# Two staging buffers instead of four for the output pass, and a reordered scale row in the layer norm

## What is computed

```python
xn = layernorm(x)
# attention branch
q, k, v = split(xn @ w_qkv.T + b_qkv)          # 16 heads of 64
kv  = einsum('bhnd,bhne->bhde', softmax(k, axis=-2), v)
out = layernorm(einsum('bhnd,bhde->bhne', silu(q), kv)) * ln_g + ln_b
out = out * sigmoid((xn @ w_g1.T + b_g1) @ w_g2.T + b_g2)
attn = out @ w_out.T + b_out
# expert branch: 8 experts, top 2 of xn @ Wr.T, capacity 769 tokens
ffn = sum over the two chosen experts of weight * (xn @ We[e])
y = x + attn + ffn
```

## Time and profile before

| | |
|---|---|
| runs before | 1159.05 us median of 3 (1157.73 to 1199.94) |
| the profiled execution | 1157.35 us |
| its span, slowest core (6) | 1155.5 us, cores 1149.5 to 1155.5 |
| TensorE busy | 873.5 us, 76% of the span |
| VectorE, ScalarE, GpSimd busy | 39%, 9%, 5% |
| experts, start to last matmul | 695 to about 1138 us |
| first store to the end | 1089.44 to 1155.5 us |

### The profile page before, as it was taken

The page is one execution under the profiler, slowest core; times in us unless marked ns, Lnnn a source line. Parts: engine busy times, 40 slices in busy tenths (PEclk is TensorE's granted clock), DMA queues, the critical chain, the costliest instruction groups (busy, mean ns, idle before and its releaser), DMA issues.

```text
span 1155.5 us, 11082 instructions; the slowest of 8 cores (1149.5 to 1155.5 us)
## 1 busy us (share of the span) xinstructions
PE 873.5 (76%) x3848; PEld 357.2 (31%) x3914; DVE 449.6 (39%) x692; ACT 103.6 (9%) x123; POOL 57.9 (5%) x58
## 2 busy tenths in 40 slices
PE   0143072599997999651555999999999999999993
PEld 0010021133335433110101334444444444444441
DVE  0123767300332001736685334444444444444441
ACT  0111100122000221141221000000000000000000
POOL 2100000000000000000000000000000000000253
PEclk9986576699997899575556999999999999999997
DMA  2566600000404002200001004040404132231176
GB/s 48 115 173 152 106 1 1 1 1 1 73 1 74 1 1 35 39 0 0 1 0 55 19 1 73 1 73 1 73 5 69 21 54 33 41 49 24 49 234 227
DMA packets 23300, 55.59 MB, mean 48 GB/s; under 512 B 4752, under 2 KB 4752, under 8 KB 22224
## 3 DMA queue, kind: packets, MB, share of 16 engines
q0 software_dynamic: 16160, 29.68, 16.1%
q1 hardware_dynamic: 4208, 12.63, 3.7%
q10 hardware_dynamic: 2880, 12.58, 2.9%
HBM read 76.18 MB, written 8.39 MB: 73 GB/s over the span
## 4 chain that ended last, share of the span: by engine, by line
PE 62%; DVE 17%; DMA 13%; issue 4%; ACT 2%; DVEq 1%; POOL 0%; POOLq 0%; ACTq 0%
PE PS L168 62%; DMA ar<-x_fm 6%; DVE scr_b L178 5%; DVE ar L178 5%; DVE srow L178 3%; DMA y<-bpool 2%; DMA y<-reps 1%; DMA y<-fpool 1%; DVE reps L178 1%; ACT bpool L185 1%; DMA wg_sb<-wg_t 1%; ACT qrow L185 1%; DVEq L177 1%; DVE qrow L178 0%; DVE drow L178 0%
## 5 line engine op out<-in xcount | busy, mean ns | idle before, releaser
L168 PE MATMUL PS<-ar 128*128 128x512 bf16 (+1 forms) x3135 | 698.8, 377 | 21.2 <-DVE ar L178 9.8
L168 PEld LDWEIGHTS PS<-ar 128*128 128x128 bf16 x3200 | 302.6, 99 | 382.8 <-issue 53.1
L178 DVE SCALAR_TENSOR_TENSOR ar<-PS,lc,ar 128x512 bf16<-128x512 f32 x256 | 192.2, 751 | 251.1 <-PE PS L168 251.1
L178 DVE CAST ar<-PS 128x512 bf16<-128x512 f32 x96 | 66.4, 692 | 168.9 <-PE PS L168 165.7
L168 PE MATMUL PS<-ar,ones_c_b 128*1 128x512 bf16 x64 | 22.3, 484 | 91.4 <-ACT bpool L185 91.1
L185 ACT ACTIVATE ar<-PS 128x512 bf16<-128x512 f32 x64 | 38.2, 597 | 94.4 <-PE PS L168 94.4
L199 POOL DMA_DIRECT2D ar<-we x8 | 7.0, 876 | 663.0 <-PE PS L168 663.0
L168 PE MATMUL PS<-bpool,wg_sb 64*128 64x512 bf16 x32 | 18.7, 584 | 28.0 <-DVE ar L178 28.0
L168 PEld LDWEIGHTS PS<-ar,ones_c_b 128*1 128x1 bf16 x64 | 5.2, 92 | 106.9 <-issue 104.5
L185 ACT ACTIVATE bpool<-ar 128x2048 bf16<-128x2048 bf16 x16 | 30.6, 1910 | 84.9 <-DMA ar<-x_fm 40.0
L168 PE MATMUL PS<-bias_b,ones_b 1*128 1x512 bf16 x96 | 37.3, 389 | 0.3
(11 more groups left out here) (113 smaller groups left out, 304.3 us busy)
## 6 DMA issues: line engine op xcount, KB each, us to landing
ar<-we POOLq DMA_DIRECT2D x8, 2048.0 KB, 16.7
fpool<-x_fm SPq DMA_DIRECT2D x4, 1024.0 KB, 9.9
ar<-x_fm POOLq DMA_DIRECT2D x8, 512.0 KB, 7.1
bpool<-x_fm ACTq DMA_DIRECT2D x4, 1024.0 KB, 7.0
bpool<-x_tm SPq DMA_DIRECT2D x8, 512.0 KB, 4.2
y<-bpool ACTq DMA_DIRECT2D x8, 512.0 KB, 3.9
ar<-wk_t POOLq DMA_DIRECT2D x1, 2048.0 KB, 16.5
ar<-wv_t POOLq DMA_DIRECT2D x1, 2048.0 KB, 15.3
```

What stands on the lines that cost most here:

```text
L168: i = eng.matmul(out, l, r, start=start, stop=stop)
L178: getattr(eng, name)(*a, **k).then_inc(S["dv"], 1)
```

## The change

The output pass has two staging buffers, `fpool` and a new tensor `fpool2` of its own, in place of four. All distances of 4 tiles become 2: the load of tile tc waits for the add of tc - 2, the add of tile tc for the store of tc - 2. The first load waits for the end of the router's use of `fpool` only. In stage 1 `fpool2` takes the f32 slices that `bp1f` took.

`erow` is gone. The row phase computes mean * r in f32 into `qrow` and then -1 times it into `crow`; TensorE makes the columns from `crow` while it holds the mean, and the sign is put in as `nmu_c` is read. In the first norm the columns wait only for r, the write of `crow` waits for the columns, and the second four steps of `reps` wait for `crow`. `totr` and `offr` lie in `srow`, and the memset of `offr` moves from the program's start to a place after the first norm on GpSimd.

```diff
+        fpool2 = sb("fpool2", [128, 2048], F32)
-        bp1f = bpool1[:].rearrange("p a b -> p (a b)").bitcast(F32)
...
-        erow = sb("erow", [1, T], BF16)
...
-        totr = sb("totr", [1, NT * E], F32)
-        offr = sb("offr", [1, NT * E], F32)
+        totr = srow[0:1, 0:NT * E]
+        offr = srow[0:1, NT * E:2 * NT * E]
...
-                gps("memset", eps_sb[:], EPS, inc=False)
-                t_const_gp = gps("memset", offr[:, 0:E], 0.0)
+                t_const_gp = gps("memset", eps_sb[:], EPS)
...
-                    fbuf = fpool[:, :] if h % 2 == 0 else bp1f
+                    fbuf = fpool[:, :] if h % 2 == 0 else fpool2[:, :]
...
                 dve("reciprocal", srow[:], qrow[:], inc=False)
-                dve("tensor_copy", drow[:], srow[:], inc=False)
-                dve("tensor_scalar_mul", erow[:], crow[:], -1.0, inc=False)
-                t_rows = dve("tensor_mul", crow[:], erow[:], drow[:])
-                w("tensor", "dv", t_rows)
+                t_r_bf = dve("tensor_copy", drow[:], srow[:])
+                w("tensor", "dv", t_r_bf)
...
-                    mm(bank(2)[:, NT + tc:NT + tc + 1], erow[0:1, 128 * tc:128 * (tc + 1)],
+                    mm(bank(2)[:, NT + tc:NT + tc + 1], crow[0:1, 128 * tc:128 * (tc + 1)],
                        ones_b[0:1, 0:1], start=True, stop=True, inc=(tc == NT - 1))
                 t_cols_pe = c["pe"]
+                dve("tensor_mul", qrow[:], crow[:], drow[:], inc=False)
+                w("vector", "pe", t_cols_pe)
+                t_rows = dve("tensor_scalar_mul", crow[:], qrow[:], -1.0)
                 w("vector", "pe", t_cols_pe)
                 dve("tensor_copy", r_c[:], bank(2)[:, 0:NT], inc=False)
-                t_cols_ev = dve("tensor_copy", nmu_c[:], bank(2)[:, NT:2 * NT])
+                t_cols_ev = dve("tensor_scalar", nmu_c[:], bank(2)[:, NT:2 * NT],
+                                -1.0, None, op0=ALU.mult)
...
+                        if which == 1 and tb == 0:
+                            w("tensor", "dv", t_rows)
...
+                w("gpsimd", "dv", t_r_bf)
+                t_offz = gps("memset", offr[0:1, 0:E], 0.0)
...
+                w("vector", "gp", t_offz)
                 dve("tensor_copy", totr[:], bank(6)[0:1, 0:128], inc=False)
...
-                dve("tensor_scalar_mul", erow[:], crow[:], -1.0, inc=False)
-                t_rows2 = dve("tensor_mul", crow[:], erow[:], drow[:])
+                dve("tensor_mul", qrow[:], crow[:], drow[:], inc=False)
+                t_rows2 = dve("tensor_scalar_mul", crow[:], qrow[:], -1.0)
...
-                pbs = (fpool[:, :], bp1f, repsf, bp2f)
+                pbs = (fpool[:, :], fpool2[:, :])
...
                 w("sync", "dv", t_lgt_hl)
-                w("sync", "pe", t_lrawT_pe)
-                w("sync", "pe", t_st2_pe)
-                w("sync", "dv", t_zg)
...
-                    pb = pbs[tc % 4]
-                    if tc >= 4:
-                        w("sync", "gp", add_toks[tc - 4])
+                    pb = pbs[tc % 2]
+                    if tc >= 2:
+                        w("sync", "gp", add_toks[tc - 2])
...
-                    if tc >= 4:
-                        w("gpsimd", "d3", out_toks[tc - 4])
+                    if tc >= 2:
+                        w("gpsimd", "d3", out_toks[tc - 2])
```

More of the change, by code:

```diff
@@ L762, in program @@
                 t_moe = c["dv"]
-                repsf = reps[:].rearrange("p a b -> p (a b)").bitcast(F32)
-                bp2f = bpool2[:].rearrange("p a b -> p (a b)").bitcast(F32)
-                pbs = (fpool[:, :], bp1f, repsf, bp2f)
+                pbs = (fpool[:, :], fpool2[:, :])
                 out_toks = {}
```

## The result

The changed kernel takes 1163.25 us (median of 11 runs), the kernel before 1158.48 us beside it; the ratio is 1.0046, 95% interval 1.0033 to 1.0059, so +5.3 us (+3.8 to +6.8). The forecast was 1163.5 us, made of +5.9 us. The profiled execution has a span of 1159.9 us on its slowest core (4); the cores lie between 1151.8 and 1159.9.

The account below looks back on a forecast made before the run. The output pass was taken as bound by its store queue, one transfer in flight; -0.2 + 0.4 + 1.6 + 4.1 = +5.9 us on the profiled 1157.35 us gave 1163.3, forecast as 1163.5 us, range 1157.0 to 1170.5.

Parts of the forecast that it names:

- The start, -0.2: GpSimd's queue of small loads: one memset leaves ahead of its first transfer, -0.2 us, ends -0.6 and 0.
- First norm, +0.4: First norm's rows: 3.41 us become 3.80, with a 2.28 us product covering TensorE's columns, +0.4 us.
- Second norm, +1.6: Second norm: same exchange of rows with nothing to cover it while TensorE waits for `crow`, +1.6 us.
- Rival four: Norms: the product costs 1.21 us, giving 1161.2 us; its chance is counted in the forecast's 0.53.
- Sum ahead of the pass +1.8: Start and both norms, before the output pass: -0.2 + 0.4 + 1.6 = +1.8 us.
- Two more stores with a load beside them, +3.1: Output pass: two more stores take 4.51 us beside a load instead of 2.98 alone, +3.1 us.
- The coupling, +1.0: Output pass: slow transfers that four buffers took up must be passed on by two, +1.0 us, between 0 and 3.1.
- The check from the other side: Output pass: 14 loads in a row lead to an end at 1157.2, the stores to 1158.5; chains meet within 1.3 us.
- Two buffers suffice for the mean durations: Output pass: load and store each have 2.2 us to spare, so the store queue stays the bound.
- rival three: Output pass: one buffer's load, add and store fall in series, +23.6 us, in all 1182.8 us; chance 0.04.
- The first two `x_tm` loads early, the rows in `srow`, `fpool2` in stage 1, costed at 0: Router rows and stage 1: loads start near 197 us without other transfers, rows and `fpool2` keep sizes; cost 0.
- lockstep: Output pass: add k releases load k + 2 and often store k together, +12.2 us, in all 1171.4 us; chance 0.16.

Follow-up runs that it names:

- Norm_bf16: Changed kernel with the product of mean and r written as bf16, not f32, in both norms: ratio 1.0017, +2.0 us against the kernel before.
- norm_only: Changed kernel with the four staging buffers and distances of 4 put back: ratio 1.0018, +2.1 us against the kernel before.
- late_loads: Kernel before, four buffers kept, but the loads of tiles 2 and 3 wait for the adds of tiles 0 and 1: ratio 1.0024, +2.8 us.
- the two experiments with fewer loads: Adds in place: changed kernel's two buffers as four slots, ratio 1.0018; kernel before's four buffers as eight slots, ratio 0.9952, both against the kernel before.
- tail_only: Kernel before with two staging buffers in the output pass and nothing else changed: ratio 1.0033, +3.8 us.
- two_stores: Kernel before with stores on two counters in turn, so two may be in flight: ratio 0.9967, -3.8 us.
- after_two_both: Changed kernel, still two buffers, with two loads and two stores in flight: ratio 1.0003, +0.3 us against the kernel before.
- two_both: Kernel before with two stores and two loads in flight, two counters on each queue: ratio 0.9925, -8.7 us.

## Why the prediction was right

Step by step, by the terms of the sum:

- The start, -0.2: the first transfer is issued at 3.13 us and not at 3.33. Right; what of it reaches the end was not measured.
- First norm, +0.4: 3.41 us became 3.80. Second norm, +1.6: TensorE's wait went from 33.58 to 35.18. Right to 0.1 us, since the product took the 2.28 us of the row with the same result type. Norm_bf16 shows that the type is the cause. Rival four is out.
- Sum ahead of the pass +1.8: the first add is 1.7 us later on the mean core, and norm_only costs +2.1 us (+0.8 to +3.4). Counted from the first `reciprocal`, four kernels with the changed norms reach the first add after 962.7 to 963.2 us and four with the norms of before after 960.5 to 961.1: 2.3 us for the 2.0 of the two norms.
- Two more stores with a load beside them, +3.1: 14 stores at 4.52 us and two short ones. Right as a mechanism by late_loads and by the two experiments with fewer loads.
- The coupling, +1.0: not found. On all eight cores the first 14 stores follow one another with no gap over 0.4 us, and from the first issue to the last landing they take 4.39 us each on average, where the first 12 took 4.43 before (in tail_only 14 take 4.46). On core 4 the pass of 71.2 us is 2.9 us over the 68.3 us of core 6 before, which the 3.1 us cover alone. The step that was oversized is the estimate of what a slow load does; the spare time worked out just before it (2.2 + 2.2 us) was the better guide, and loads on core 4 were not slow, 4.9 us at most against 6.0 on core 6 before. By the times of late_loads and tail_only alone it could still be 1 us or a little more; by the store rows it is 14 x 0.03 = 0.4 us.
- The check from the other side, that the loads' chain nearly meets the stores': it does not bind here, but it was the right thing to look at, for it is what stopped two_stores.
- "Two buffers suffice for the mean durations": right, as long as one transfer at a time is in flight, and wrong in after_two_both. The series of rival three, priced with load, add and store, did not occur; what occurs with full queues is the shorter round of add and store.
- The first two `x_tm` loads early, the rows in `srow`, `fpool2` in stage 1, costed at 0: nothing in norm_only beyond the norms' own 1.8 us.

The forecast's 1163.5 us also rests on a little luck: +1.0 for the coupling is too much, and the forecast notes that the median of the runs lies 1.7 us above the profiled execution but then adds 0.2 us to the sum for it. With the 1.7 it would have been 1165.0, so the two slips partly cancel. One reading was off without an effect: against lockstep it gives the later stores beside loads 4.4 us on average, and the stores of tiles 2 to 11 took 4.2, which speaks against that rival a little more.

## What to carry to other kernels

Before counting buffers, ask how many transfers a queue has in flight. With one at a time, as here, the waits between buffers were hidden behind the queue, and what fewer buffers really cost was the early loads that they pushed into the busy stretch. Price it by the same transfer's two durations, alone and in company, which the tail of one profile shows side by side. And where a row on one partition is on the path, the type of an intermediate result counts as much as the number of instructions: take the price from the row whose result has the same type.

## What was not expected of the hardware

- On core 6 of the kernel before, loads of 512 KB take 3.5 to 4.0 us to land with nothing beside them, stores 2.6 to 3.2, and with one of each in flight their medians are 4.2 and 4.3. With two of each in flight (two_both) the medians differ by core, 4.9 to 6.6 us for loads and 5.2 to 6.4 for stores. From 1100 to 1130 us cores 0, 4 and 6 move 228 to 247 GB/s before and 295 to 303 in two_both, where I had feared that 260 was the limit.
- The cores fall in two groups long before the pass: the first `reciprocal` starts mostly at 120 to 123 us on some and at 124 to 127 on others. In each of the twelve profiles every pair of neighbours (cores 0 and 1, 2 and 3, 4 and 5, 6 and 7) has one early and one late core, 3.4 to 8.1 us apart, and which of the two is early changes from kernel to kernel. The slowest core is a late one in all twelve, and this scatter in the loading of x is larger than most terms argued here. Its cause was not looked into.
